# A decoder layer on one core: GpSimd's wide work in the first stage moved to VectorE

## The reference

```python
def bitlinear(x, w, g):            # both weights are rounded to -1, 0, 1 times a mean
    xn = x * rsqrt(mean(x**2) + 1e-6) * g
    scale = 127.0 / clip(max(abs(xn), axis=-1), 1e-5)
    xq = clip(round(xn * scale), -128, 127) / scale
    return xq @ weight_quant(w).T

x = x + bitlinear(gate * sigmoid(gate) * v, w_down, g_down)   # gate, v = split(bitlinear(layernorm(x), w_gate, g_gate)), 1408 columns each
x = x + xattn(layernorm(x))        # one of 4 experts by token
x = x + ffn(layernorm(x))          # shared part and top 2 of 8 experts
```

## Time and profile before

| | us |
|---|---|
| median of 3 runs | 934.32 |
| lowest and highest | 933.33, 942.64 |
| span of the profiled execution | 967.5 |

### The profile page before, as it was taken

How to read it: one execution, slowest core, us unless ns; L and a number is a source line. 1 busy time by engine, 2 the same in 40 slices (tenths; PEclk the granted TensorE clock), 3 DMA queues, 4 the chain that set the end, 5 groups by cost and what they waited for, 6 DMA issues and landing times.

```text
span 967.5 us, 17562 instructions
## 1 busy us (share of the span) xinstructions
PE 760.4 (79%) x5001; PEld 452.5 (47%) x5017; DVE 504.4 (52%) x861; ACT 397.7 (41%) x567; POOL 263.6 (27%) x401
## 2 busy tenths in 40 slices
PE   0457777777429999749778998899999999999275
PEld 0234443444215555335445655566666666665133
DVE  6779888887714555446564567222222222222146
ACT  5866556656515555335343543122332223231010
POOL 1235665565321111032121000111111111104710
PEclk9979899888559999969898999899999999999679
DMA  9312222212544555267776542122222222226843
GB/s 353 112 34 77 61 70 87 87 66 87 158 159 135 180 179 179 95 209 238 230 215 216 201 148 78 56 88 87 76 77 86 87 78 77 84 77 224 248 138 138
DMA packets 51204, 127.57 MB, mean 132 GB/s; under 512 B 6496, under 2 KB 6496, under 8 KB 50528
## 3 DMA queue, kind: packets, MB, share of 16 engines
q1 hardware_dynamic: 42688, 99.33, 30.5%
q0 software_dynamic: 8480, 27.79, 9.9%
HBM read 87.78 MB, written 39.32 MB: 131 GB/s over the span
## 4 chain that ended last, share of the span: by engine, by line
PE 47%; DMA 10%; issue 4%; another core or an unknown queue 4%; DVE 4%; SPq 2%; ACT 1%; POOL 0%; DVEq 0%; POOLq 0%; ACTq 0%
PE banks L1338 41%; DMA x_d<-w_hi 5%; PE banks L1330 3%; PE banks L1428 2%; DMA x_d<-yrow 2%; DMA hC_d<-w_lo 1%; PE banks L1360 1%; DMA rows<-hC_d 1%; DVE w_hi L1246 0%; DMA rows<-hC_d,idx 0%; SPq L458 0%; SPq L441 0%; DVE w_lo L1102 0%; DMA rows<-hB_d,idx 0%
## 5 line engine op out<-in xcount | busy, mean ns | idle before, releaser
L1338 PE MATMUL banks<-w_hi,hT 128*128 (+1 forms) x1288 | 321.0, 326 | 4.4 <-issue 3.2
L1338 PE MATMUL banks<-w_lo,hT 128*128 (+1 forms) x644 | 209.8, 326 | 0.0
L1338 PEld LDWEIGHTS banks<-w_hi,hT 128*128 128x128 f16 x1288 | 128.0, 99 | 82.2 <-issue 10.6
L1338 PE MATMUL banks<-w_hi,cpT 128*128 (+1 forms) x426 | 142.9, 390 | 10.0 <-issue 8.6
L1299 PE MATMUL banks<-w_hi,w_lo 128*128 128x352 bf16 x384 | 89.3, 350 | 45.6 <-DVE w_hi L1015 34.3
L844 ACT ACTIVATE cs<-banks 128x352 f32<-128x352 f32 x71 | 32.9, 463 | 201.7 <-PE banks L1338 175.5
L1160 DVE TENSOR_TENSOR cs<-banks,cs 128x352 f32<-128x352 f32 x71 | 37.1, 523 | 140.9 <-ACT cs L844 135.0
L1164 DVE TENSOR_TENSOR cpT<-banks,cpT 128x384 f16<-128x384 f32 x71 | 39.5, 556 | 129.3 <-ACT cpT L849 112.6
L1338 PE MATMUL banks<-w_lo,cpT 128*128 (+1 forms) x213 | 83.1, 390 | 5.3 <-issue 5.3
L1330 PE MATMUL banks<-eyeH,rows 128*128 128x128 f16 x584 | 47.6, 225 | 48.2 <-DMA rows<-hC_d 19.6
L1338 PEld LDWEIGHTS banks<-w_lo,hT 128*128 128x128 f16 x644 | 63.9, 99 | 34.5 <-issue 0.8
(11 more groups left out here) (191 smaller groups left out, 1214.3 us busy)
## 6 DMA issues: line engine op xcount, KB each, us to landing
wstage<-in_wmoe SPq DMA_DIRECT2D x40, 544.0 KB
yC_d<-yrow SPq DMA_DIRECT2D x39, 256.0 KB, 2.0
w_hi<-x_d SPq DMA_DIRECT2D x20, 256.0 KB
yB_d<-yrow SPq DMA_DIRECT2D x19, 256.0 KB, 2.0
w_hi<-in_wgate SPq DMA_DIRECT2D x3, 1408.0 KB, 9.9
w_hi<-in_x SPq DMA_DIRECT2D x16, 256.0 KB, 2.8
w_lo<-in_x SPq DMA_DIRECT2D x16, 256.0 KB, 3.6
x_d<-w_lo SPq DMA_DIRECT2D x16, 256.0 KB, 2.9
```

The lines of the kernel that those rows point to most:

```text
L1338: mm = pe.matmul(to, a(k, pa), w(k, pw), start=(begins and k == 0 and n == 0), stop=(ends and k == steps - 1 and n == 2))
```

## The change

The products with the gains and the subtraction for the low half leave GpSimd, whose list keeps the three groups of 128x1 operations. VectorE does both: the product in one instruction of 1408 columns instead of two of 704, and both steps between `swiglu(3)` and `x_absmax`.

```diff
--- before.py
+++ after.py
@@ -586,16 +586,6 @@
                 alone(pool, "pool", x_max, s.t + 1)
                 pool.tensor_scalar(w[:, 2:3], xmax[s.u][:], w[:, 1:2], EPS_Q, ALU.mult, ALU.max).then_inc(smA_s, 1)
 
-            def gains(s, half):
-
-                at = slice(half * IA // HALVES, (half + 1) * IA // HALVES)
-                alone(pool, "pool", sw_done, s.t * CA + (half + 1) * CA // HALVES)
-                before(pool, d_q, s.t, 2)
-                pool.sem_inc(passed["pool"], 1)
-                if isinstance(s.t, int) and s.t == 0:
-                    pool.wait_ge(gd_in, 16)
-                pool.tensor_tensor(swg[s.u][:, at], sw[s.u][:, at], gd[:, at], ALU.mult).then_inc(swg_done, 1)
-
             def small_g(s):
 
                 w, n0 = smG[s.u], s.t * 3
@@ -614,14 +604,7 @@
                 alone(pool, "pool", mo1, s.t + 1)
                 rsqrt_chain(smB_s, s.t, mv1[:, 1:2], EPS_LN, var1[:], rstd1[:], rs1)
 
-            def h_lo(s):
-                alone(pool, "pool", hi_done, s.t + 1)
-                before(pool, hb_out[s.u], s.h, 1, 16)
-                pool.sem_inc(passed["pool"], 1)
-                pool.tensor_tensor(rows[s.u][:, D:2 * D], hA, rows[s.u][:, 0:D], ALU.subtract).then_inc(lo_done, 1)
-
-            pipeline(pool, T, [(-2, small_x), (1, small_g), (3, small_b), (0, lambda s: gains(s, 0)),
-                               (0, lambda s: gains(s, 1)), (3, h_lo)])
+            pipeline(pool, T, [(-2, small_x), (1, small_g), (3, small_b)])
 
 
             def gather(s, order, done, index, inv, dst, table, t0=0):
@@ -1010,13 +993,25 @@
                 dve.wait_ge(sil_done, s.t * CA + (c + 1))
                 if c == 0:
                     before(dve, sq_done, s.t, 2)
-                    before(dve, swg_done, s.t, 2, HALVES)
+                    before(dve, swg_done, s.t, 2)
                     dve.wait_ge(x_dq, s.t + 1)
                 dve.scalar_tensor_tensor(out=sw[s.u][:, c * CW:(c + 1) * CW], in0=bank(2 + c % 2, CW), scalar=dqx[s.u][:],
                                          in1=sil[c % 2], op0=ALU.mult, op1=ALU.mult).then_inc(sw_done, 1)
 
+            def gains(s):
+                dve.wait_ge(sw_done, (s.t + 1) * CA)
+                before(dve, d_q, s.t, 2)
+                if isinstance(s.t, int) and s.t == 0:
+                    dve.wait_ge(gd_in, 16)
+                dve.tensor_tensor(swg[s.u], sw[s.u], gd, ALU.mult).then_inc(swg_done, 1)
+
+            def h_lo(s):
+                dve.wait_ge(hi_done, s.t + 1)
+                before(dve, hb_out[s.u], s.h, 1, 16)
+                dve.tensor_tensor(rows[s.u][:, D:2 * D], hA, rows[s.u][:, 0:D], ALU.subtract).then_inc(lo_done, 1)
+
             def g_absmax(s):
-                dve.wait_ge(swg_done, (s.t + 1) * HALVES)
+                dve.wait_ge(swg_done, s.t + 1)
                 before(dve, g_small, s.t, 2)
                 dve.tensor_reduce(gmax[s.u][:], swg[s.u], AX.X, ALU.max, apply_absolute_value=True).then_inc(g_max, 1)
 
@@ -1060,7 +1055,8 @@
             stages = [(3, residual1), (0, lambda s: swiglu(s, 0)), (1, g_absmax), (-3, x_spread),
                       (0, lambda s: swiglu(s, 1)), (-1, x_int), (3, spread1), (-3, x_moments), (-2, x_reciprocal),
                       (3, moments1), (-2, x_factor), (0, lambda s: swiglu(s, 2)), (1, g_reciprocal), (3, norm1),
-                      (1, g_factor), (-3, x_center), (0, lambda s: swiglu(s, 3)), (-3, x_absmax), (1, d_int)]
+                      (1, g_factor), (-3, x_center), (0, lambda s: swiglu(s, 3)), (3, h_lo), (0, gains), (-3, x_absmax),
+                      (1, d_int)]
             pipeline(dve, T, stages, end=-1)
```

## The result

The changed kernel takes **956.8 us** (median of 3 runs, 952.0 to 959.4) against 934.3: ratio 1.0206, 95% interval 1.0129 to 1.0283. Forecast were 949, with a range of 936 to 960, and slower at 0.70.

What follows compares the result with a forecast made beforehand. No engine was full: a loop through all engines bounds the round, with VectorE deciding its second half. Rounds 9.7 + start 1.3 + end 4.0 = 15.0 us on 934.3 gave 949 us, range 936 to 960.

Steps and rivals of the forecast that it cites:

- parts a and b: VectorE per round: norm1 and d_int shorten by 2.62 us together; added h_lo (0.69) and gains (1.62) add 2.17 us.
- part c: VectorE waits 0.90 us ahead of h_lo for ScalarE's h_hi; round +0.53 us at upper clock, +1.09 at lower.
- The mis-sized term: Rounds 3 to 14 of the first stage: mean loss 0.81 us over 12 rounds, +9.7 us, bounds 6.4 and 13.1.
- (d): Start of the first stage, rounds 0 to 2: +1.3 us for the three together, bounds 0 and +2.2.
- (e): End of the first stage: ctx pieces behind h_lo on VectorE make the last store later, +4.0 us, bounds +2 and +6.
- (f): GpSimd's 128x1 order and VectorE's waits on it stay; later stages pass the delay of their start through undiminished.
- (1): First-stage rounds: VectorE's busy time decides, no wait ahead of h_lo, -0.45 us a round, 929 us; chance 0.12.
- (2): TensorE's clock falls oftener, every round of the slower kind, 14.44 us, total 956 us; chance 0.15 together with (3).
- the sign given for it: For (2): TensorE's gate matmuls at the lower clock level in every round.
- (3): GpSimd's small_x operations block norm1, x_center and d_int; loop grows by 0.56 us, 956 us; chance 0.15 together with (2).
- (4): End of the stage not carried over, or sizes cancel: 7.4 us in all, 942 us, no difference; chance 0.18.
- The rule weighed against a row: norm1 beside GpSimd: the skill's "fully blocks" gives a gain of 1.60 us, the row 1.33; by the rule 946 us.

Runs made afterwards that it cites:

- the exchange on ScalarE: The changed kernel with h_hi put ahead of d_round in ScalarE's list; ratio 0.9985 to the kernel before.
- the best order here: The changed kernel with gains moved behind the next round's swiglu(0), ahead of g_absmax, and h_lo behind d_int; ratio 0.9822 to the kernel before.

## Why the prediction was right

*The bound and the durations* (parts a and b) held to 0.01 us: `norm1` 0.55, `d_int` 0.88, `gains` 1.62, `h_lo` 0.69.

*The wait* (part c) was the right step and nearly the right size in the middle: walked 0.90 us idle and rounds of 13.9 on the mean; measured 0.89 us idle in rounds 7 to 11 and 1.11 to 1.28 in the others up to 14, with rounds of 13.8 to 13.9 from 6 to 11 (14.0 to 14.25 in 3 to 5). Rounds 3 to 11 lost 0.88 us each against the 0.81 taken. That the wait is the cause, and not the work, is shown three ways: it goes with the exchange on ScalarE (0.9985), it comes back without any work (1.018 from 0.9912), and it can be moved behind `d_int` (0.9927).

*The mis-sized term* is that mean applied to twelve rounds. Rounds 12 to 14 lost 1.66, 1.60 and 1.50 us. From round 13 on VectorE has no `x_center` (the tiles three ahead are used up); before, that shortened the round from 12.85 or 13.36 to 12.06, but after, with the path by way of ScalarE, only from 13.9 to 13.6. Round 12 takes 15.02 us: TensorE stays at the lower level (1.2 GHz) past the gate into `down`, which takes 3.8 us instead of 2.5 in round 11, so that `silu(3)` and with it `d_round` and `h_hi` come late. The granted clock over rounds 11 and 12:

```profile
190.45:204.34 13.89, 9.72 (x58) 5.67 (x58) 11.30 (x23) 8.03 (x13) 3.32 (x9) 0.87 0.17 58
204.34:219.36 15.02, 11.25 (x58) 6.15 (x58) 11.40 (x23) 7.92 (x13) 3.31 (x9) 0.80 0.15 52
```

So rounds 3 to 14 cost 12.7 us and not 9.7. (The forecast's own range had a slip as well: 934.3 + 8.4 is 942.7, where it says 944.)

*The start* (d) cost 2.3 us at the end of round 2, not 1.3, just beyond the upper bound of 2.2. ScalarE waited 3.55 us for `winv` instead of 1.88, as forecast, and round 0 ended 1.9 us late. In round 1 `gains` came (+1.55) and `d_int` gave its gain (2.11 to 0.88), but that of `x_center` (1.91 to 0.74) was lost: VectorE stood 1.71 us ahead of `swiglu(3)`, for a `silu(3)` that TensorE's gate matmuls released late. So round 1 ended 2.9 us late, and round 2 gave 0.6 back.

*The end* (e): rounds 15 to 18 took 3.6 us more, against 4.0. The mechanism is shown by the pieces put ahead of `h_lo`, which gain 5.8 us: their place costs more than the whole term. Something in the change makes part of it up; no run takes these apart, so that the size came out near 4.0 is in part luck.

*The later stages* (f) passed the delay on: 18.6 us at the store, 20.0 at the last expert sum. The 1.4 us between I didn't trace. Sum: 12.7 + 2.3 + 3.6 = 18.6 us, where 15.0 were forecast. The medians of three runs each differ by 22.5 us; 2 of these are that before's own median over 24 runs is 936.3.

*The rivals.* (1) VectorE's busy time decides: refuted by its fall from 46.3 to 42.1 us in a slower kernel; but it named the right point. Once ScalarE's `h_hi` is early, the rounds change by -0.42 us, where this rival's sum had -0.45; the start (1.7 us) and the end (1.0) take half of it back, and the kernel is no slower than before. (2) The clock: the sign given for it did come. Each round from 5 to 12 after starts its gate matmuls at 1.06 to 1.09 us for three, where before only every other did. Its 956 us is also nearer to the measured 956.8 than the forecast is, but that is luck: it counted twelve rounds of 14.44 us, and rounds 6 to 11 took 13.8 to 13.9. The level goes with the wait, and I had put it as one or the other. Before, a round that starts at the lower level takes 0.5 us more (13.36 against 12.85), and round 12 after is a clear case of its cost; the mean granted clock of the stretch hardly moves (0.86 to 0.87). No run holds the clock fixed, so its share of the 12.7 us stays open. (3) GpSimd's 128x1 work in the way: `x_center` 0.74 and `norm1` 0.55 throughout, so no. The contention is there, but it is GpSimd that waits: its third `small_x` operation takes 0.76 us beside `d_int` instead of 0.30. (4) An end that isn't carried over: refuted by the 20.0.

My expectation of 946 us for the exchange had this same mistake: it took away the visible wait only, and not the end of the stage, where the last `d_int` period falls from 13.44 to 11.97 as well. In rounds 3 to 12 the exchange gained 1.42 us a round, where the wait was 1.07 on the mean. The level is one part of the rest (rounds 4, 7 and 11, at the upper level through the whole gate, take 12.3 us, the others 12.6 to 12.9); what else is in it I didn't trace.

*The rule weighed against a row.* `norm1` gave 1.33 us, as the row said. The Trainium skill's SBUF — State Buffer, "Who interferes with whom", would have had 1.60 of it by "fully blocks"; the measured difference stays with the row.

## What to carry to other kernels

When a step moves to another engine, its wait moves too: ask who stands behind it in the new queue, and put it there behind whatever releases the other engines. Busy time is no measure of such a move: here the busiest engine was relieved by 0.4 us a round and the kernel became 2% slower. If a wide GpSimd operation starts just ahead of VectorE's critical ones, what moving it can win at most is the whole contention (2.9 us a round here), and the order decides how much of it one gets (1.3 in rounds 3 to 12 of the best order here): the same two steps on VectorE gave ratios from 0.982 to 1.021 by their place alone.

## What the runs showed of the hardware

A 128x1 operation of GpSimd, L587, takes 0.30 us alone, 0.76 beside `d_int`, 1.28 beside `d_int` with `h_lo` behind it, and 2.49 beside `d_int` with `gains` behind it. In the last two cases it ended 0.1 us after the second VectorE instruction: it was not let in between the two.

Two inputs from memory contend too: VectorE's subtraction took 0.69 us alone and 1.61 beside a GpSimd product. `swiglu`, with one input from `banks` and one from memory, stayed at 0.55 to 0.58 in every run. The Trainium skill, SBUF — State Buffer, "Who interferes with whom", says that a two-input instruction of VectorE contends with a GpSimd instruction that reads, and one with at most one such input outside its two-port modes doesn't; the rows agree with both.

TensorE's level alternated from round to round before, was the lower at the first gate matmuls of rounds 5 to 12 after, and with rounds of 11.82 us it was the upper throughout (granted clock 1.00 from 90 to 210 us). The idle time just ahead doesn't tell it: TensorE's turn ran at the lower level (1.35 us) after 0.25 us idle before, and at the upper (0.79) after 2.05 with the products alone moved. What it costs can be read there too: with the products alone moved, rounds 4, 7 and 10 kept the upper level through the gate and took 12.2 us; 5, 8 and 11 started at the lower and took 12.5 to 12.6; in 3, 6, 9 and 12 it fell within the gate, and they took 12.8.
